# Row maximum and scaling of an attention softmax: a reduce and a multiply against one multiply-and-minimum per head

## The reference

```python
scores = jnp.einsum('bhqd,bhkd->bhqk', q, kj) * SCALE
scores = jnp.where(causal[None, None], -jnp.inf, scores)   # the first attention only
chunk_max = scores.max(axis=-1, keepdims=True)
exp_c = jnp.exp(scores - new_m)                            # new_m is the row maximum here
new_s = exp_c.sum(axis=-1, keepdims=True)
out = einsum(exp_c / new_s, v)
```

## Time and profile before

| | |
|---|---|
| median of 3 runs | 1507.68 us (1507.03 to 1513.49) |
| profiled execution | 1504.07 us, span 1502.3 us |
| busy: PE, DVE, ACT, POOL | 1330.9, 964.9, 927.6, 519.0 us |
| row maximum L344 | 256 times, 158.4 us busy |
| scaling L346 | 256 times, 48.2 us busy |
| exponentials L312 | 512 times, 225.1 us, and 107.8 us of accumulator reads |

### The profile page before, as it was taken

How to read it: one execution, slowest core, us unless ns; L and a number is a source line. 1 busy time by engine, 2 the same in 40 slices (tenths; PEclk the granted TensorE clock), 3 DMA queues, 4 the chain that set the end, 5 groups by cost and what they waited for, 6 DMA issues and landing times.

```text
span 1502.3 us, 37766 instructions
## 1 busy us (share of the span) xinstructions
PE 1330.9 (89%) x11005; PEld 837.6 (56%) x11006; DVE 964.9 (64%) x2381; ACT 927.6 (62%) x2269; POOL 519.0 (35%) x532
## 2 busy tenths in 40 slices
PE   4888888958989999999999999677989899898987
PEld 3665566624656666666666666344555555565553
DVE  5888888664545566555655633244787786877764
ACT  4877777724656666666666666334766667566653
POOL 1045444565324433431000001665554554442000
PEclk9999999979999999999999999988999999999999
DMA  2044444469788766766676545766655645543000
GB/s 73 29 176 183 156 148 148 178 231 315 270 288 288 262 224 237 264 215 231 229 236 219 184 146 152 131 105 89 103 83 80 107 67 89 96 69 70 2 15 29
DMA packets 96149, 233.42 MB, mean 155 GB/s; under 512 B 11824, under 2 KB 11824, under 8 KB 91440
## 3 DMA queue, kind: packets, MB, share of 16 engines
q0 software_dynamic: 33712, 113.79, 30.4%
q1 hardware_dynamic: 62336, 118.34, 23.6%
HBM read 140.84 MB, written 91.24 MB: 154 GB/s over the span
## 4 chain that ended last, share of the span: by engine, by line
PE 44%; DMA 10%; DVE 8%; issue 7%; ACT 3%; POOL 3%; SPq 2%; DVEq 0%; POOLq 0%; ACTq 0%
PE bank L1329 18%; PE bank L1353 10%; PE bank L1586 6%; DMA xs<-y_tiles,slot_ix 6%; PE bank L1317 4%; POOL xs L449 2%; PE bank L277 2%; DMA xg<-x_slots 2%; PE bank L1340 1%; PE bank L297 1%; PE bank L1592 1%; DVE l_nmax L344 1%; DMA x_slots<-blank 1%; ACT l_probs L312 1%; PE bank L259 1%
## 5 line engine op out<-in xcount | busy, mean ns | idle before, releaser
L1329 PE MATMUL bank<-wh,xT 128*128 x1280 | 340.3, 328 | 6.2 <-DVE hp L1445 4.1
L449 POOL DMA_INDIRECT xs<-y_tiles,slot_ix x120 | 192.3, 1603 | 238.2 <-DMA y_tiles<-ysb 98.9
L312 ACT ACTIVATE l_probs<-bank,l_bias 128x256 f32<-128x256 f32 (+1 forms) x512 | 225.1, 451 | 59.5 <-DVE l_bias L346 58.8
L1329 PE MATMUL bank<-wl,xT 128*128 x640 | 209.7, 328 | 0.0
L344 DVE TENSOR_REDUCE l_nmax<-bank 128x2 f32<-128x512 f32 (+1 forms) x256 | 158.4, 619 | 66.6 <-PE bank L259 38.8
L1435 DVE SCALAR_TENSOR_TENSOR hv<-bank,sg 128x192 f32<-128x192 f32 x160 | 57.0, 356 | 222.9 <-ACT sg L1389 200.6
L1404 ACT ACTIVATE ysb<-bank,xg 128x512 f32<-128x512 f32 x160 | 109.9, 687 | 118.3 <-PE bank L1353 118.3
L324 ACT ACTIVATE l_probsT<-bank 128x512 f32<-128x512 f32 (+1 forms) x256 | 140.8, 550 | 67.1 <-PE bank L297 66.7
L1383 ACT ACTIVATE xT<-bank 128x1024 f16<-128x1024 f16 x160 | 162.6, 1017 | 14.2 <-PE bank L1317 13.8
L1329 PEld LDWEIGHTS bank<-wh,xT 128*128 128x128 f16 x1280 | 125.6, 98 | 81.3 <-issue 11.1
L1353 PE MATMUL bank<-wh,hT 128*128 x480 | 156.3, 380 | 0.9 <-issue 0.6
(11 more groups left out here) (249 smaller groups left out, 2580.9 us busy)
## 6 DMA issues: line engine op xcount, KB each, us to landing
xg<-x_slots SPq DMA_DIRECT2D x160, 272.0 KB, 2.8
y_tiles<-ysb SPq DMA_DIRECT2D x160, 256.0 KB, 2.5
raw<-in_experts_dram POOLq DMA_DIRECT2D x30, 1280.0 KB, 7.2
x_slots<-blank SPq DMA_DIRECT2D x33, 272.0 KB, 5.2
xs<-in_x_dram SPq DMA_DIRECT2D x8, 512.0 KB, 4.7
cbuf<-in_ctx_dram SPq DMA_DIRECT2D x8, 512.0 KB, 5.7
stage<-in_mats_dram POOLq DMA_DIRECT2D x4, 1024.0 KB, 7.7
room<-in_ctx_dram SPq DMA_DIRECT2D x8, 512.0 KB, 5.1
```

What stands on the lines that cost most here:

```text
L312: last = self.nc.scalar.activation(self.probs[:, s % 2, u, 0:nk], self.pS[s % 2][:, u * S : u * S + nk], ACT.Exp, bias=self.bias[:, s % 4, ...
L449: return nc.gpsimd.indirect_dma_start(to, None, self.y_tiles[0 : (MT + 1 - k) * P, :], ix, compute_op=ALU.add)
L1329: last = nc.tensor.matmul(bGU[t.place % 2][:, 0:GU], xT[:, t.place % 2, xo + c * P : xo + (c + 1) * P], wp[:, bass.ds(w, 1), c * GU : (c + ...
```

## The change

The reduce over both heads and the small multiply are replaced by two VectorE operations, one per head. Each multiplies the head's scores by the negated scale, takes the minimum of that and a huge number (which changes nothing), writes the products to a new tile `scaled` that nobody reads, and puts the minimum of the row in its accumulator output, which goes straight to `bias`. The minimum of the negated scores is the negated maximum, so `bias` holds the same numbers. The semaphore `max_made` goes. A new wait on `bias_made` for the step two before guards the reuse of `scaled`.

```diff
@@ class Attention, __init__
-        self.nmax = sb(tag + "nmax", [P, 4, 2])
+        self.scaled = sb(tag + "scaled", [P, 2, 2, S])
-        self.scores_made, self.max_made, self.bias_made = sem(tag + "scores"), sem(tag + "max"), sem(tag + "bias_s")
+        self.scores_made, self.bias_made = sem(tag + "scores"), sem(tag + "bias_s")
@@ dve_max
         dve.wait_ge(self.scores_made, STEPS * b.n + s + 1)
-        v = self.pS[s % 2][:, :].rearrange("p (u k) -> p u k", u=2)[:, :, 0:nk]
-        self.nc.vector.tensor_reduce(self.nmax[:, s % 4, :], v, AX, ALU.max).then_inc(self.max_made, 1)
-        dve.wait_ge(self.max_made, STEPS * b.n + s + 1)
-        self.nc.vector.tensor_scalar(self.bias[:, s % 4, :], self.nmax[:, s % 4, :], -self.scale, None, ALU.mult).then_inc(self.bias_made, 1)
+        if s >= 2 or not (isinstance(b.n, int) and b.n == 0):
+            dve.wait_ge(self.bias_made, STEPS * b.n + s - 1)
+        for u in range(2):
+            last = self.nc.vector.tensor_scalar(self.scaled[:, s % 2, u, 0:nk], self.pS[s % 2][:, u * S : u * S + nk], -self.scale, HUGE,
+                                                ALU.mult, ALU.min, accum_out=self.bias[:, s % 4, u : u + 1])
+        last.then_inc(self.bias_made, 1)
```

More of the change, by code:

```diff
@@ L46 @@
 SC_N = 2.0**10
+HUGE = 3.0e38
 SC_C = 2.0**8
```

## The result

| | before | after |
|---|---|---|
| median of 20 executions each | 1505.33 us (1500.32 to 1514.43) | 1497.68 us (1491.33 to 1506.83) |
| profiled execution, span | 1502.3 us | 1494.6 us |

The ratio is 0.9947, with a 95% interval of 0.9929 to 0.9965. The change gains 8 us, 5.3 to 10.7 us. The forecast was a loss of about 6 us, and the time lies just under the low end of its range. The cost is that of rival 1, "the accumulator costs nothing of its own", to which I had given 0.12; the accumulator does have an instruction of its own, which that rival did not expect.

What follows compares the result with a forecast made beforehand. DVE and PE were taken to bound layer 0, mainly PE layer 1. +0.052 us a step on 113 path steps made +5.9 us: 1510.0 us for the profiled execution, 1513 on the median, range 1498 to 1536.

Steps and rivals of the forecast that it cites:

- rival 1: VectorE's accumulator output costs nothing of its own: -0.11 us a step, -12 us on the path, 1495.6 us; chance 0.12.
- the cost of the accumulator read: Getting each head's minimum out of VectorE's accumulator was put at 0.08 us, twice a step, between nothing and 0.17.
- The lower bound: Least cost per head of VectorE's accumulator output: nothing, if the main operation writes the minimum itself.
- the three signs: Forecast wrong if there is no separate accumulator read, it costs over 0.1 us, or the main operation is much longer.
- The main operations: VectorE's two multiply-and-minimum operations per step: 422 or 290 ns long, costing 0.34 us (256 columns) or 0.21 (128).
- the 0.11 us that were read for the wait: The small multiply's wait for the reduce on VectorE, about 0.11 us a step, which the change takes away.
- The new wait on `bias`: VectorE's wait for the bias of two steps before: put at 0, at most 0.02 us a step, 2 us in all.
- the products are stored: The store of products into `scaled` runs beside the PSUM read and costs nothing more.
- DVE's busy time in L347: Busy time of main operations and accumulator reads was to rise from 206.6 us for the old pairs to about 285.
- Rival 3: No overlap on VectorE, each operation starting after the one before ends: +0.39 us a step, +44 us, 1552; chance 0.08.
- The multiplier: Steps counted as on the path, which multiply DVE's change per step: 81 in layer 0 plus 32 in layer 1, 113 of 256.
- Counting how often the chain of waits passes through the reduce in one batch: Layer 1's path steps: four passes in the batch from 1151 to 1212 us, 32 steps over 8 batches.

Runs made afterwards that it cites:

- Run 5: Changed kernel with two multiply-and-minimum operations without accumulator between each step's two, `scaled` in 16 bits: 1619.49 us (one execution); kernel before on that chip 1550.01.
- run 4: Changed kernel with one unrelated small VectorE addition (about 0.1 us) behind each step's pair: 1505.28 us, ratio 0.9991 to the kernel before.
- run 12: Kernel before with one negated reduce per step writing `bias`, no multiply, softmax scale moved into the query and key factors (a repeat): 1486.67 us, ratio 0.9869.
- run 10: Changed kernel with 0.40 us of VectorE work behind the pair in layer 0's six steps where ACT waits for the bias: 1509.01 us, ratio 1.0012 to before.
- run 11: Changed kernel with 0.40 us of VectorE work behind the pair in layer 0's steps 5 to 8, where neither engine waits: 1508.06 us, ratio 1.0017 to before.
- run 2: Changed kernel with the new pair in layer 1 alone, old reduce and multiply in layer 0: 1502.53 us, ratio 0.9975 to the kernel before.
- run 1: Changed kernel with the new pair in layer 0 alone, old reduce and multiply in layer 1: 1502.69 us, ratio 0.999 to the kernel before.
- run 9: Changed kernel with 0.40 us of VectorE work behind the pair in layer 0's six steps where DVE waits for scores: 1496.86 us, ratio 0.9933 to before.
- run 3: Changed kernel with one unrelated small VectorE addition (about 0.1 us) ahead of each step's pair: 1508.06 us, ratio 1.0016 to the kernel before.

## Why the prediction was wrong

**The step that failed** is the cost of the accumulator read, in the prediction's words "I take 0.08 us, since these are the nearest in kind". Run 5 gives about 0.01, and in the timeline of the changed kernel a main operation with its read takes no longer than the 0.21 and 0.34 us forecast for it alone. Twice a step, this one term turns -0.11 us into +0.05. The lower bound that I had written down, "nothing", was the truth, but I took it for the case of a main operation that writes the minimum itself. In fact there is a separate read, and it lies wholly beside the end of its main operation. The neighbours that I leaned on were operations with columns of their own to pass, and ACT's read, which costs 0.09 us. They do not stand for DVE's read. None of the three signs that the prediction named for its being wrong came true (no separate read, a read over 0.1 us, a long main operation): a read that costs next to nothing was not among them.

**What held.** The main operations were within 4 ns, in cost as in duration: 0.34 and 0.21 us. A step is shorter by the 0.11 us that were read for the wait, and run 4 gives the gain back by filling just that much. No run takes the wait away alone; run 12 takes wait and multiply away together, 0.20 us with 128 keys. The new wait on `bias` costs nothing, since a main operation starts with the read ahead of it also where its step begins anew (203.36 in the timeline). That the products are stored as well costs nothing visible. The read costs little in the record too. DVE's busy time in L347 is 146.5 + 42.2 + 31.3 = 220.0 us, where 285 was forecast. Of the 65 us between them, 45 are the reads (42.2 instead of 512 x 0.17 = 87) and 20 are a slip of counting: the two main operations of a step overlap in the record by 0.08 us, and busy time counts that once (384 x 0.419 is 160.9 us, and the row says 146.5). DVE's whole busy time fell, from 964.9 to 943.4 us, where the prediction had it rise.

**The overlap.** The Trainium skill, VectorE: DVE Perf Modes, section The DRAIN you can't avoid, says that "the next op does not start until the 8-stage pipe empties", and the prediction quoted it so. The section goes on: "A next op that is not held starts earlier". With that sentence it agrees with both traces, where the next operation starts 0.08 us before the recorded end of the one before; the tiles of these operations fill all 128 partitions and so start at 0, and by the section that it points to, Two Vector instructions with no wait between them, none of these operations is held. Rival 3, built on the first sentence alone, would have given 1552 us. The section also says that "the semaphore costs nothing extra here", of eight copies. For an operation that waits for the result of the one before it, this trace disagrees: the multiply starts 0.03 us after the reduce has ended, and not 0.08 before, which makes 0.11 us.

**The multiplier** was near in sum and wrong in its parts. With a read of 0 the prediction's sum is 113 x -0.107 = -12 us, and -8.0 was measured (interval -10.7 to -5.3). In the two traces the two layers gained 5.5 + 4.6 = 10.1 us, worth 94 steps, and TensorE's clock took a part back:

- Layer 0 gave 5.5 us by its last landmark, worth 5.5 / 0.107 = 51 steps, not 81. In runs 10 and 11 the same steps pay 27.5 us for 10 x 8 x 0.40 = 32 us. So they are on the path for a delay, but a saving soon meets another limit. DVE's waits for scores show it: 25.5 us before, 32.9 after, and 39.0 in run 12 with its still shorter steps.
- One such limit can be read directly. POOL computes `rstd` from `mv`, and DVE's next piece `room` needs it:

```profile
203.09 0.71 POOL L711 TENSOR_TENSOR rstd<-mv,neghalf 128x2 f32<-128x2 f32 x1 [3.58 <-DVE mv L748]
```

  It ends at 203.80, and `room` starts at 203.84, 0.05 us after the last main operation had let go at 203.79. In the earlier trace rows `room` came straight behind the pair. In run 12 the wait is 0.18 us:

```profile
200.08 0.75 DVE L345 TENSOR_REDUCE l_bias<-bank 128x2 f32<-128x256 f32 x2
201.01 1.00 DVE L747 TENSOR_SCALAR room<-xs,mv,rstd 128x512 f32<-128x512 f32 x2 [0.18 <-POOL rstd L707]
```

  In the changed kernel this is 8 x 0.05 = 0.4 us of the 3 that are missing. I did not find a single place for the others; that they lie in the longer waits for scores is argued, not shown.
- Layer 1 gave 4.6 us, 5.2 in run 2: 43 to 49 steps, not 32. Counting how often the chain of waits passes through the reduce in one batch was too low.
- Between the end of layer 0 and the start of the experts, this execution lost 2.4 us: from the last landmark of layer 0 until DVE writes `t_free`, which the experts' rows wait for, it is 19.4 us, against 17.0 before. The cause is TensorE's clock. First the two stretches, before and after (busy us of PE, PEld, DVE, ACT, POOL with instructions, granted clock, DMA), then TensorE's rows in each:

```profile
301.50:318.50 17.00, 10.60 (x65) 6.06 (x64) 10.75 (x36) 5.50 (x14) 10.31 (x12) 1.00 0.39 153
296.00:315.40 19.40, 14.53 (x65) 8.57 (x65) 10.93 (x37) 5.53 (x14) 10.65 (x12) 0.74 0.36 142
...
312.17 1.97 PE L678 MATMUL bank<-gw,room 128*128 128x32 f32 x16 [0.69 <-ACT room L704]
313.98 1.89 PE L100 MATMUL bank<-id 128*128 128x512 f16 x8
316.62 0.18 PE L684 MATMUL bank<-chosen,tri 128*128 128x32 f16 x1 [0.75 <-DVE chosen L776]
...
307.16 3.62 PE L681 MATMUL bank<-gw,room 128*128 128x32 f32 x16 [0.69 <-ACT room L707]
310.59 3.60 PE L101 MATMUL bank<-id 128*128 128x512 f16 x8
313.98 0.23 PE L687 MATMUL bank<-chosen,tri 128*128 128x32 f16 x1
```

  The same matmuls run at 2.4 GHz before and at 1.2 GHz after. From the start of the sixteen to the matmul of `chosen` it is 4.45 us before and 6.82 after, 2.4 more. In all the runs on these chips the clock tells the two lengths apart. Runs 1, 2 and 9 have 19.3 or 19.4 us with a granted clock of 0.74, run 2 with layer 0 as it was before. Runs 3, 4, 10 and 11 have 17.0 or 17.1 us at 1.00, and run 12 17.1 at 0.89, where the fall comes only at the end. So the new pair is not what takes the time. Whether it makes the clock fall sooner in more of the executions is not shown. Before the fall PE did the same in both kernels: seventeen of the L100 matmuls in 3.83 us, then 2.3 us idle for `room`.
- The 1.6 us lost at the very end go the same way. From layer 1's last landmark to the end it is 24.7 us at a granted clock of 1.00 (before, runs 3 and 11) and 26.2 to 27.4 us at 0.85 to 0.94 (after, and all the others of these chips).

Together: -5.5 + 2.4 = -3.1 at the start of the experts, -4.7 at layer 1's first landmark, -9.3 at its last, and -7.7 at the end. The 1.6 us in the experts mean nothing: the same instructions take 723.2 to 727.1 us there in these ten profiles. Whether the median gain of 8 us falls short of these 10 for the same reason is not shown: it is read from this one pair of executions only.

**The chances.** Rival 1 had the right cost and 0.12. The doubt about the read was a doubt in one number with known ends, 0 and 0.17, and its condition for faster, a read under about 0.02 us, deserved more than 0.12, since only an accumulator read on another engine and operations of another kind stood against it. That the measured time came so near the low end of the range, 1498, is luck: a read of 0 and 113 steps make 1495.6.

## What to carry to other kernels

Do not add up recorded durations: read the cost of an instruction from its start to the start of the next. On VectorE an accumulator output added about 0.01 us here, while waiting for one's own result cost 0.11 us by the timeline, so a fused operation pays even where it passes no fewer columns, and leaving the second operation out altogether (run 12) saves nearly twice as much a step, 0.20 us. To find which steps count, delay chosen groups of them (runs 9 to 11): neither the list of an engine's waits nor one chain gave the right weight, and a saving may be worth less than the same delay costs. Before a difference of a few us between two profiles is put down to an edit, look at the granted clock of each stretch, and compare single batches at the same clock.

## What the runs showed of the hardware

- VectorE's read of an accumulator is recorded with 82 ns and costs 7 to 17 (run 5); ScalarE's is recorded with 0.20 us and costs 0.09.
- A reduce with negated output takes the same 685 and 420 ns as one without.
- A multiply with minimum over fp32 in PSUM takes 419 ns for 256 columns and 286 for 128, and costs 0.34 and 0.21 us, with or without an accumulator.
- Sixteen 128x32 matmuls of 32 bits took 1.97 us at 2.4 GHz and 3.62 us at 1.2 GHz; the fall of the clock made the stretch behind layer 0 2.4 us longer with the same instructions.
- One chip took 1550.0 us for the kernel before, others 1505 to 1506, and the ratio of the change was the same on it (0.9948 and 0.9947).
